# One block's adapter back in float32, both halves of two others from float32r parts

## The reference

```python
h = x * (scale[:, None, :] * rsqrt(mean(x*x) + EPS))
val, gate = split(h @ up_w.T)                 # 2 x 2048 wide
h = val * gelu(gate)
y = act_quant(h) @ weight_quant(down_w).T + x # one step per token, one for the weight
Wd_b = Wd + 0.1 * reshape(cond @ Wdd.T + bdd) # per sequence, 128 x 512
Wu_b = Wu + 0.1 * reshape(cond @ Wdu.T + bdu) # per sequence, 512 x 128
out = y + relu(y @ Wd_b.T + bd) @ Wu_b.T + bu
```

## Time and profile before

| | |
|---|---|
| median of 3 runs | 839.31 us (838.85 to 839.36) |
| profiled execution | 840.44 us, span 838.7 us |
| PE busy | 821.2 us, 98% of the span |
| DVE busy | 664.3 us, 79% |
| ACT busy | 399.8 us, 48% |
| POOL busy | 121.3 us, 14% |
| chain that ended last | PE 85%, DVE 5%, issue 3% |

### The profile page before, as it was taken

How to read it: one execution, slowest core, us unless ns; L and a number is a source line. 1 busy time by engine, 2 the same in 40 slices (tenths; PEclk the granted TensorE clock), 3 DMA queues, 4 the chain that set the end, 5 groups by cost and what they waited for, 6 DMA issues and landing times.

```text
span 838.7 us, 11856 instructions
## 1 busy us (share of the span) xinstructions
PE 821.2 (98%) x3914; PEld 359.4 (43%) x3914; DVE 664.3 (79%) x968; ACT 399.8 (48%) x653; POOL 121.3 (14%) x91
## 2 busy tenths in 40 slices
PE   5999999999999999999999999999999999999998
PEld 4334444444344334444444444444444444444443
DVE  5998787889878889767787678988986586675986
ACT  5778887776454532227445543326433333324000
POOL 0363332302001153300101011100200000001000
PEclk9999999999999999999999999999999999999999
DMA  9879989666899862377798865337247435435232
GB/s 343 338 257 347 343 289 297 233 217 226 303 347 366 330 218 95 136 271 272 280 326 303 304 223 191 116 95 255 72 137 239 138 95 189 138 95 176 101 125 76
DMA packets 64860, 186.65 MB, mean 223 GB/s; under 512 B 7072, under 2 KB 8352, under 8 KB 64416
## 3 DMA queue, kind: packets, MB, share of 16 engines
q1 hardware_dynamic: 64512, 185.63, 63.5%
q10 hardware_dynamic: 288, 0.26, 0.1%
HBM read 154.41 MB, written 30.41 MB: 220 GB/s over the span
## 4 chain that ended last, share of the span: by engine, by line
PE 85%; DVE 5%; issue 3%; ACT 1%; DVEq 0%; ACTq 0%
PE b_ps L1351 9%; PE b_ps L1355 9%; PE b_ps L1353 9%; PE aux_ps L1406 6%; PE a_ps L1351 6%; PE aux_ps L1464 6%; PE a_ps L1355 6%; PE a_ps L1353 6%; PE c_ps L1351 3%; PE aux_ps L1542 3%; PE e_ps L1351 3%; PE e_ps L1355 3%; PE e_ps L1353 3%; PE c_ps L1353 3%; PE c_ps L1355 3%
## 5 line engine op out<-in xcount | busy, mean ns | idle before, releaser
L1954 DVE SCALAR_TENSOR_TENSOR h_ring<-v_sb,unscale,gelu 128x512 f32<-128x512 f32 x63 | 55.5, 881 | 58.0 <-ACT gelu L1092 31.9
L1351 PE MATMUL b_ps<-t_mov,u_l 128*128 128x512 f16 x252 | 95.5, 379 | 3.8 <-DVE c_ps L1915 3.6
L1355 PE MATMUL b_ps<-t_mov,u_l 128*128 128x512 f16 x252 | 95.5, 379 | 0.0
L1353 PE MATMUL b_ps<-t_mov,u_l 128*128 128x512 f16 x252 | 95.5, 379 | 0.0
L1978 DVE TENSOR_TENSOR hmax<-gelu,hmax 128x512 f32<-128x512 f32 x120 | 88.6, 740 | 7.8 <-ACT gelu L1098 2.9
L1068 ACT ACTIVATE b_ps<-a_ps 128x512 f32<-128x512 f32 x63 | 36.7, 582 | 94.1 <-PE a_ps L1355 93.9
L1102 ACT ACTIVATE gelu<-h_ring 128x512 f32<-128x512 f32 x64 | 40.3, 629 | 67.6 <-DVE h_ring L1954 67.6
L2013 DVE TENSOR_TENSOR h_ring<-h_ring,qscale 128x1024 f16<-128x1024 f32 x48 | 64.7, 1387 | 0.0
L1084 ACT ACTIVATE gelu<-a_ps,unscale 128x512 f32<-128x512 f32 x64 | 43.7, 682 | 43.3 <-DVE hmax L1978 41.1
L916 POOL PARTITION_ALL_REDUCE yscale<-hmax x8 | 17.9, 2266 | 321.0 <-DVE hmax L1978 320.3
L1098 ACT ACTIVATE gelu<-h_ring 128x512 f32<-128x512 f32 x64 | 40.2, 628 | 45.6 <-DVE h_ring L1964 45.3
(11 more groups left out here) (264 smaller groups left out, 1701.4 us busy)
## 6 DMA issues: line engine op xcount, KB each, us to landing
w_ring<-in_Wdu SPq DMA_DIRECT2D x64, 512.0 KB, 6.0
w_ring<-in_Wdd SPq DMA_DIRECT2D x56, 512.0 KB, 7.2
u_l<-ul_dram SPq DMA_DIRECT2D x48, 512.0 KB, 4.7
u_e<-ue_dram SPq DMA_DIRECT2D x48, 384.0 KB, 3.2
h_ring<-in_up_w SPq DMA_DIRECT2D x16, 512.0 KB, 6.4
x_sb<-in_x SPq DMA_DIRECT2D x8, 1024.0 KB, 7.9
res<-in_down_w SPq DMA_DIRECT2D x16, 512.0 KB, 7.1
ul_dram<-u_l SPq DMA_DIRECT2D x15, 512.0 KB, 5.6
```

What stands on the lines that cost most here:

```text
L1351: pe.matmul(ps[:, :], weight(n, p, 0, k), hi, start=fresh and k == 0, stop=False, skip_group_check=True)
L1353: pe.matmul(ps[:, :], weight(n, p, 0, k), lo, start=False, stop=False, skip_group_check=True)
L1355: mm = pe.matmul(ps[:, :], weight(n, p, 1, k), hi, start=False, stop=k == 1, skip_group_check=True)
L1954: dve.scalar_tensor_tensor(out=h_slot(n)[:, TB:TS], in0=val[:, :], scalar=unscale[:, s // 2, j:j + 1], in1=gelu2[:, :], op0=ALU.mult, op1= ...
```

## The change

Block 0's adapter runs in float32 in both halves. Blocks 1 and 2 run both halves from float32r parts, so their down half needs parts of the down weights and of the blocks' rows too. `weight_high` makes both high parts of the weights on ACT in quad 49; the low parts follow on DVE, the down weights' in quad 51, the up weights' in quad 53. The rows of block 1 are copied by ACT at the end of quad 50, in two halves, and their low parts made by DVE in quad 51. Those of block 2 are copied at the end of quad 53, behind the gelu (first half), and in quad 54 (second half), with the low parts in quads 54 and 55. A row copy waits for the block's load and for the down half that last read `x_parts`. `x_parts` shares the memory of `x_sb`, so the loads of x for the end move from quads 50 and 53 to quads 56 and 57 and wait for block 2's down half. In the last super-block the chunks of `quantise` are spread by a table of its own: none at j = 3, three at j = 5 and at j = 8. The semaphores of two early copies are merged into `s_first_hi` and `s_first_lo`, with the same waits.

```diff
 QUANTISE = {3: 2, 4: 2, 5: 2, 6: 2, 7: 2, 8: 2, 9: 2, 10: 1}
+QUANTISE_LAST = {4: 2, 5: 3, 6: 2, 7: 2, 8: 3, 9: 2, 10: 1}
 Y_FIRST = 10
...
 NEXT_X = {2: 0, 5: 1}
+LAST_X = {56: 0, 57: 1}
...
 MID_AT = {49: 0, 52: 1, 55: 2}
-SPLIT = len(MID_AT)
+SPLIT = (1, 2)
+LAST_SPLIT = 2
+X_LOW = {51: ((1, 0), (1, 1)), 54: ((2, 0),), 55: ((2, 1),)}
 UP_AT = {n + 1 + k // 2: (i, (k, k + 1)) for n, i in MID_AT.items() for k in (0, 2)}
+def part_at(i):
+    return (0, 2, 4)[i]
...
             mid_parts = first.enter_context(nc.sbuf_tensor("mid_parts", [P, 2, TB], F32R))
+            x_parts = first.enter_context(nc.sbuf_tensor("x_parts", [P, 2, KD, TB], F32R))
         res = sb("res", [P, 4, TB])
         stage = sb("stage", [P, 2, TB])
+        x_sb = sb("x_sb", [P, 2, KD, TB])
         u_e = sb("u_e", [P, 2, 2, 768], F16)
         u_l = sb("u_l", [P, 2, 2, 1024], F16)
         t_mov = sb("t_mov", [P, 7, 2, 2 * TB], F16)
         h_ring = sb("h_ring", [P, SLOTS, TS])
-        x_sb = sb("x_sb", [P, 2, KD, TB])
         wq = sb("wq", [P, NP, D], F8)
...
                 "p5": (s_x1, 2 * KD * i + 6 + key[-1] + 1),
-                "mid": (s_part_lo, at + 2) if at < SPLIT else (s_relu, at + 1),
+                "mid": (s_part_lo, part_at(i)) if i in SPLIT else (s_relu, at + 1),
                 "up": (s_out, KD * at + key[-1] + 1),
...
-                if s:
+                if s == NSB:
+                    aux_ready(sp, "mid", LAST_SPLIT)
+                elif s:
                     sp.wait_ge(s_tlo, 7 * s + 1)
...
                     load_l(n + 1)
-                if j in NEXT_X:
+                if s + 1 < NSB and j in NEXT_X:
                     load_x(s + 1, NEXT_X[j])
+                if n in LAST_X:
+                    load_x(s + 1, LAST_X[n])
                 if s == 1 and Y_FIRST <= j < Y_FIRST + 4:
...
                 act.wait_ge(s_x_c22, 2 if at < 3 else 4)
-                if at >= SPLIT:
+                if i not in SPLIT:
                     act.activation(stage[:, at % 2, :], bank("mid", i)[:, :], ACT.Relu,
                                    bias=bd_sb[:, 0:1]).then_inc(s_relu, 1)
                     return
                 act.activation(bank("mid", i)[:, :], bank("mid", i)[:, :], ACT.Relu,
                                bias=bd_sb[:, 0:1]).then_inc(s_relu, 1)
                 act.wait_ge(s_relu, at + 1)
-                if at:
-                    aux_ready(act, "up", ADAPTERS[at - 1], KD - 1)
+                aux_ready(act, "up", i - 1, KD - 1)
                 act.activation(mid_parts[:, 0, :], bank("mid", i)[:, :], ACT.Copy)\
                     .then_inc(s_part_hi, 1)
-            def up_weight_high():
+            def weight_high():
                 act.wait_ge(s_l1w, 3)
                 for h in range(2):
                     act.wait_ge(s_res_put[h], 16 * 6)
+                    act.wait_ge(s_c22_put[h], 16)
+                act.activation(up_parts[:, 2, :], l1_wd[:, 0, :, :].rearrange("p k n -> p (k n)"),
+                               ACT.Copy).then_inc(s_part_hi, 1)
                 act.activation(up_parts[:, 0, :], l1_wu[:, 0, :], ACT.Copy).then_inc(s_part_hi, 1)
+            def x_high(i, halves=(0, 1)):
+                act.wait_ge(s_ad[i % 2], 16 * (i // 2 + 1))
+                if i == 1:
+                    act.wait_ge(s_tlo, split_count(NSB - 1, T4))
+                else:
+                    aux_ready(act, "mid", i - 1)
+                for half in halves:
+                    rows = slice(2 * half, 2 * half + 2)
+                    act.activation(x_parts[:, 0, rows, :], ad_slot(i)[:, rows, :], ACT.Copy)\
+                        .then_inc(s_x_hi, 1)
...
                 absolute1(n - 1)
+                if n == 54:
+                    x_high(2, (1,))
                 if j == 0 or n == 1:
...
                     stage_group(g)
-                if n == NQ - NP - 2:
-                    up_weight_high()
+                if n == 49:
+                    weight_high()
+                if n == 50:
+                    x_high(1)
+                if n == 53:
+                    x_high(2, (0,))
                 if n in MID_AT:
...
                     pe.wait_ge(s_ad[i % 2], 16 * (i // 2 + 1))
+                if i in SPLIT:
+                    pe.wait_ge(s_part_lo, 1)
+                    for k in range(KD):
+                        if k % 2 == 0:
+                            pe.wait_ge(s_x_lo, 2 * i - 1 + k // 2)
+                        hi, lo = (up_parts[:, 2 + n, P * k:P * k + P] for n in range(2))
+                        x_hi, x_lo = (x_parts[:, n, k, :] for n in range(2))
+                        pe.matmul(ps[:, :], hi, x_hi, start=(k == 0), stop=False)
+                        pe.matmul(ps[:, :], hi, x_lo, start=False, stop=False)
+                        mm = pe.matmul(ps[:, :], lo, x_hi, start=False, stop=(k == KD - 1))
+                    mm.then_inc(s_aux, 1)
+                    return
                 for k in ks:
...
                 at = ADAPTERS.index(i)
-                if at < SPLIT:
-                    pe.wait_ge(s_part_lo, 1)
-                    pe.wait_ge(s_part_lo, at + 2)
+                if i in SPLIT:
+                    pe.wait_ge(s_part_lo, 3 if i == 1 else 4)
                     cols = slice(P * k, P * k + P)
...
+            def down_weight_low():
+                dve.wait_ge(s_part_hi, 1)
+                dve.tensor_tensor(up_parts[:, 3, :],
+                                  l1_wd[:, 0, :, :].rearrange("p k n -> p (k n)"),
+                                  up_parts[:, 2, :].bitcast(F32), ALU.subtract)\
+                    .then_inc(s_part_lo, 1)
             def up_weight_low():
-                dve.wait_ge(s_part_hi, 1)
+                dve.wait_ge(s_part_hi, 2)
                 dve.tensor_tensor(up_parts[:, 1, :], l1_wu[:, 0, :],
                                   up_parts[:, 0, :].bitcast(F32), ALU.subtract)\
                     .then_inc(s_part_lo, 1)
+            def x_low(i, half):
+                rows = slice(2 * half, 2 * half + 2)
+                dve.wait_ge(s_x_hi, 2 * i - 1 + half)
+                dve.tensor_tensor(x_parts[:, 1, rows, :], ad_slot(i)[:, rows, :],
+                                  x_parts[:, 0, rows, :].bitcast(F32), ALU.subtract)\
+                    .then_inc(s_x_lo, 1)
             def mid_low(i):
-                dve.wait_ge(s_part_hi, ADAPTERS.index(i) + 2)
+                dve.wait_ge(s_part_hi, i + 2)
                 dve.tensor_tensor(mid_parts[:, 1, :], bank("mid", i)[:, :],
...
                         x_scaled(key[1])
-                    elif key[0] == "mid":
+                    elif key[0] == "mid" and key[1] in SPLIT:
                         mid_low(key[1])
...
                     scales(s, 0)
-                if s > 0 and j in QUANTISE:
-                    first = 1 + sum(v for q, v in QUANTISE.items() if q < j)
-                    quantise(s - 1, range(first, first + QUANTISE[j]))
+                chunks = QUANTISE_LAST if s == NSB - 1 else QUANTISE
+                if s > 0 and j in chunks:
+                    first = 1 + sum(v for q, v in chunks.items() if q < j)
+                    quantise(s - 1, range(first, first + chunks[j]))
                 if s > 1 and j == 10:
                     token_sums(s - 1, 1)
                     token_sums(s - 1, 3)
+                for i, half in X_LOW.get(n, ()):
+                    x_low(i, half)
+                if n == 51:
+                    down_weight_low()
+                if n == 53:
+                    up_weight_low()
                 if n in ASSEMBLE:
...
                 val2(n)
-                if n == NQ - NP - 1:
-                    up_weight_low()
                 if n == 1:
```

More of the change, by code:

```diff
@@ L457, in build @@
         s_first_lo = sem("s_first_lo")
-        s_sums_hi = sem("s_sums_hi")
-        s_sums_lo = sem("s_sums_lo")
         s_sums_put = sem("s_sums_put")
@@ L499, in build @@
         s_out = sem("s_out")
+        s_x_hi = sem("s_x_hi")
+        s_x_lo = sem("s_x_lo")
         s_part_hi = sem("s_part_hi")
@@ L574, in put_sums @@
             def put_sums():
-                sp.wait_ge(s_sums_lo, 2)
+                sp.wait_ge(s_first_lo, 3)
                 sp.dma_start(ue_dram[0].rearrange("p (a m) -> p a m", a=2)[:, :, 256:768],
@@ L643, in load_c11 @@
                 if d == 2:
-                    aux_ready(sp, "up", SPLIT - 1, KD - 1)
+                    aux_ready(sp, "up", LAST_SPLIT, KD - 1)
                 for h in range(2):
@@ L893, in weight_sums @@
                     if j == 6:
-                        pool.wait_ge(s_sums_lo, 2)
+                        pool.wait_ge(s_first_lo, 3)
                     pool.wait_ge(s_ulo, part_count(j - 2, 3))
@@ L1029, in sums_high @@
                 act.activation(s_split(pair)[:, 0, :], s_sum(0, 2 * pair, 2 * pair + 2), ACT.Copy,
-                               scale=um_mul[:, 0:1]).then_inc(s_sums_hi, 1)
+                               scale=um_mul[:, 0:1]).then_inc(s_first_hi, 1)
```

(6 more changed lines are left out.)

## The result

The changed kernel takes 837.60 us (median of 15 runs, 836.27 to 839.44); the kernel before, on the same chip, 839.16 (15 runs). The ratio is 0.9984, 95% interval 0.9976 to 0.9992: 1.6 us less by the medians, 0.7 to 2.0 us less by the interval. So the whole time tells that the kernel is a little faster, but not which part of the change did it. Forecast was 837.5. The profiled execution took 838.22 us, its span went from 838.7 to 836.5.

What follows compares the result with a forecast made beforehand. PE was taken to bound the adapters' stretch (busy 78.86 of 78.90 us), with DVE the bound in quads 47 to 53. The terms 0.70 + 0.60 + 0.48 - 0 = 1.8 us took 839.31 to 837.5, range 837.0 to 839.3.

Steps and rivals of the forecast that it cites:

- Step 1: PE, adapters of blocks 0 to 2: three float32r part matmuls replace one float32 matmul's 0.86 us with 0.69; net 0.7 us gained.
- rival of another rate: PE's part matmuls step at 0.216 us (gain 2.0, 837.3) or 0.24 (gain 1.7, 837.6); chance 0.08.
- Step 2: DVE's low part of the up weights leaves quad 47; 0.6 of PE's 0.79 us of waits in quads 48 and 49 returns.
- Step 3: Block 0's low part leaves DVE in quad 50; PE's wait before that quad's last product goes, 0.48 us.
- Step 4: DVE's added low parts in quads 51 to 56 cost PE 0, bounds 0 and 0.3; tightest is quad 53, slack 0.06 us.
- sign that the seed ends within 0.1 us of PE's need: Quad 53: DVE's write of c_ps (L1915) was to end within 0.1 us of when PE needs it.
- Step 5: ACT's added copies and the moved loads are free; block 2's load takes 5.8 us, landing at 644.2, before ACT's copy.
- third rival: Block 2's load is slower and holds ACT between quad 53's gelu and quad 54's L1068; 3.3 us slack; chance 0.10.
- slower case: ACT held by block 2's load: 0.2% slower, 3.5 us, needs a load of 12.6 us, giving 841; slower overall 0.07.
- best end: Best bounds of the matmul and wait terms together, 0.86 + 0.79 + 0.48 us, giving 837.2.

Runs made afterwards that it cites:

- e5: Changed kernel with all parts float16 instead of float32r: 837.02 us; first matmul of quad 47 to that of quad 58 121.03 us, changed kernel beside it 121.68.
- e1: Changed kernel with the up weights' high part back on ACT in quad 46, low part on DVE in quad 47: 838.25 us; quads 47 to 58 +0.59 us.
- e2: Changed kernel plus one unused 128x512 subtraction on DVE in quad 50: 837.62 us; quads 47 to 58 +0.50 us.
- e6: Changed kernel plus one unused 128x512 subtraction on DVE in quad 53: 839.56 us in a single run; quads 47 to 58 +0.51 us.
- e4: Changed kernel with the load of block 2's rows issued one quad later, behind quad 53's weight loads: 839.27 us; quads 47 to 58 +1.98 us.
- e3: Changed kernel with ACT's copy of block 2's first rows moved ahead of quad 53's gate2: 845.31 us; quads 47 to 58 +7.01 us.
- e7: Changed kernel with block 0's up half from float32r parts too, their low parts on DVE in quad 50: 837.07 us; quads 47 to 58 121.08 us.

## Why the prediction was right, and where it wasn't

The forecast of the whole time, 837.5 against 837.60, is closer than it deserves: runs of one kernel lie 3 us apart. What tests the prediction is the stage, 1.83 us shorter where the sum has 1.78, and within it each step in its own place.

**Step 1** said 0.69 us for three part matmuls and a net 0.7. Twelve took 2.76; 2.75 was named. By the starts of the quads, the two down halves gave 0.68 and 0.69 us, and block 0's two up pairs took 0.34 and 0.32 back: net 0.71. The price was taken from the up half, where the same form already ran, and it held in the down half. The rival of another rate falls for float32r. e5 shows that float16 parts run at that rate, 0.216, and what it would have brought.

**Step 2** said 0.6 of 0.79. It was 0.60, and e1 puts 0.59 back. The rest stayed where the step had left it: it says that 0.05 us "remain" behind the write of v_sb and 0.15 behind quad 49's seed. Its own sums make these waits, and not room: 593.55 + 0.15 is 0.07 later than 593.63. Measured are 0.05 ahead of 593.31 and 0.14 ahead of 596.04. That POOL moves along was argued from its releaser and holds: its all-reduces begin 8.72 us after the start of quad 48 instead of 9.32, 0.60 earlier, and are as long as before, 4.53 us. The low part beside them again takes 2.19.

**Step 3** said 0.48; it was 0.48, and e2 costs 0.50.

**Step 4** left quad 53 a slack of 0.06 us; it is 0.15 by the timeline and by e6. So the sign that the seed ends within 0.1 us of PE's need did not come, though no wait came either. Here the prediction was lucky in part: it put its term at 0 with 0.06 us to spare, out of durations read to 0.01. It held because each operation had a row, and because the steps between starts (0.60 and 1.13) were added and not the durations (0.68 and 1.22). With the durations the sum would have shown a wait.

**Step 5** had the load land 5.8 us after its issue. It took 5.6, and the copy follows the gelu without a wait.

What failed is a price that didn't enter the sum, that of the third rival. It gave ACT 3.3 us of slack and said "Beyond it each microsecond costs one". The slack is 4.3 us. The store ahead of the load landed after 7.5 us instead of 8.2 and the load was 0.2 shorter, which gives back what the shorter down half takes. And the price holds for 2 us of stall (e4), not for 4.8 (e3), where the clock's fall adds 2.2. So its slower case may begin before a stall of 3.5 us; no stall of a length between the two was run. The chance given to the rival isn't touched by this, but its price for a long stall was too low. The range has a slip too: it is said to leave out the best end, 837.2, but begins at 837.0 and holds it.

One thing is open: the run's time moves by 1 us and more in work that all these kernels share. At quad 47 the profiled runs of the changed kernel and its variants stand between 567.70 (e7, which explains most of its short span, 833.6) and 570.78 us (e6), the kernel before at 570.32. So the 0.37 us ahead of quad 47 can't be put down to the change. No run here says why it moves.

## What to carry to other kernels

Where one engine is busy all the time, price a moved operation by its place: 0.60 us of DVE work cost 0.45 to 0.6 us ahead of a value that the busy engine waits for (e1, e2, e6), and two such operations caused no wait behind it (e7). When the change is as small as here, under 0.3%, compare a stretch between two marks of the busy engine instead of whole runs. And when a rival is a stall, ask whether the matmul engine will be slow after it: here that added nearly half of the stall again (2.2 us to 4.8).

## What was not expected of the hardware

- A stall of 4.8 us cost 7.0: the granted clock was 0.50 behind it, while the next twelve matmuls took 4.9 us instead of 2.7. A stall of 1.9 us (e4) left the clock at 1.00 and cost 1.98.
- float32r weight loads take 0.19 us and float16 ones 0.10, yet the matmuls' steps differ by only 0.014 us.
- A 1 MB load from memory took 5.6 us with the weights' loads issued 2.7 us behind it, and 7.5 with them just ahead of it (one load each).
